# Gated edge terms for two batches at a time, and wider one-hots in the first mean pass, in a four-layer graph network

## The reference, cut to what matters

```python
x = layernorm(x + gated(x, edge_index, edge_attr_64, ...))
x = layernorm(x + mean_sage(x, ...))
x = layernorm(x + gat_twice(x, edge_index, edge_attr_128, ...))
x = layernorm(x + two_mean_layers(x, edge_index, ...))

# gated: a message for each edge, summed by target, divided by the degree
msg_in = concat([h[src], h[dst], e], -1)
m = (silu(msg_in @ w1 + b1) @ w2 + b2) * sigmoid(msg_in @ wg + bg)
agg = segment_sum(m, dst, n) / max(deg, 1)
# mean_sage
agg = segment_sum(feat[src], dst, n) / max(deg, 1)
out = feat @ W_self + b_self + agg @ W_neigh
# each of the two attention layers needs, of every edge
a_e = edge_attr_128 @ We @ att_e
```

## Time and profile before

| | |
|---|---|
| median of 3 runs | 1869.95 us (1869.58 to 1870.87) |
| the profiled execution's own time | 1871.19 us |
| its span | 1869.3 us |
| mean granted TensorE clock | 0.89 |
| TensorE busy | 1563.2 us (84%) |
| VectorE busy | 1479.7 us (79%) |
| ScalarE busy | 1148.4 us (61%) |
| GpSimd busy | 937.0 us (50%) |

### The profile page before, as it was taken

The page is one execution under the profiler, slowest core; times in us unless marked ns, Lnnn a source line. Parts: engine busy times, 40 slices in busy tenths (PEclk is TensorE's granted clock), DMA queues, the critical chain, the costliest instruction groups (busy, mean ns, idle before and its releaser), DMA issues. The chain is left out here.

```text
span 1869.3 us, 43539 instructions
## 1 busy us (share of the span) xinstructions
PE 1563.2 (84%) x13220; PEld 1350.2 (72%) x13220; DVE 1479.7 (79%) x4411; ACT 1148.4 (61%) x2906; POOL 937.0 (50%) x940
## 2 busy tenths in 40 slices
PE   6699999999999846999674899884659989479996
PEld 5488888888888733555573798784649978379995
DVE  5688888888888688999556998756689977668797
ACT  2577677777777537677310998753059976366572
POOL 4777777777777230000054777755567777300000
PEclk9799999999999967999865899996669999689897
DMA  6888888888888300232273211114621111346561
GB/s 199 246 260 247 244 253 264 256 264 256 252 251 262 115 5 36 95 128 116 101 214 74 62 40 42 42 33 126 149 57 44 41 42 42 124 151 243 200 243 37
DMA packets 148928, 273.55 MB, mean 146 GB/s; under 512 B 28039, under 2 KB 88909, under 8 KB 146436
## 3 DMA queue, kind: packets, MB, share of 16 engines
q1 hardware_dynamic: 110430, 192.44, 31.8%
q0 software_dynamic: 33408, 75.68, 15.1%
q10 hardware_dynamic: 4854, 2.55, 0.6%
HBM read 225.06 MB, written 45.51 MB: 145 GB/s over the span
## 5 line engine op out<-in xcount | busy, mean ns | idle before, releaser
L1002 POOL DMA_INDIRECT gated_rows<-p_tab,src_idx x416 | 434.9, 1045 | 152.0 <-issue 121.2
L1410 POOL DMA_INDIRECT cur<-table,src_idx x240 | 247.0, 1029 | 95.0 <-issue 54.5
L1119 ACT ACTIVATE gated_sig<-gated_pre 128x512 f32<-128x512 f32 x208 | 131.4, 632 | 153.6 <-DVE gated_pre L1207 139.8
L1622 PE MATMUL bank<-attention_counts,h_sb 128*128 128x260 f32 (+1 forms) x900 | 216.4, 364 | 0.0
L1043 PE MATMUL bank<-gated_wide_q,gated_comb 128*128 128x256 f32 x832 | 216.0, 382 | 0.0
L2335 PE MATMUL bank<-mean_wide,mean_xs 128*128 128x416 f32 (+2 forms) x900 | 182.3, 360 | 35.1 <-DVE mean_xs L2451 33.0
L1207 DVE TENSOR_TENSOR gated_pre<-bank,gated_rows 128x512 f32<-128x512 f32 x208 | 142.8, 687 | 77.2 <-PE bank L1043 76.6
L2335 PEld LDWEIGHTS bank<-mean_wide,mean_xs 128*128 128x128 f32 x900 | 165.0, 206 | 38.3 <-ACT mean_wide L2293 33.3
L1550 ACT ACTIVATE attention_lo<-attention_plain,w_left 128x128 fp32r<-128x128 bf16 x512 | 177.3, 398 | 14.1 <-DVE attention_plain L1671 13.7
L1571 ACT COPY attention_counts<-bank 128x475 f32 (+1 forms) x256 | 143.8, 562 | 63.0 <-PE bank L1610 59.5
L1605 PE MATMUL bank<-attention_wide_a,attention_lo 128*128 128x300 f32 x512 | 157.5, 391 | 18.7 <-ACT attention_lo L1550 9.6
(11 more groups left out here) (452 smaller groups left out, 4114.6 us busy)
## 6 DMA issues: line engine op xcount, KB each, us to landing
counts<-count_tabs SPq DMA_DIRECT2D x16, 2675.0 KB, 9.4
h_sb<-in_edge_attr_dram SPq DMA_DIRECT2D x51, 512.0 KB
count_tabs<-mean_counts SPq DMA_DIRECT2D x40, 535.0 KB, 2.8
gated_relr<-rel_rows SPq DMA_DIRECT2D x104, 128.0 KB
gated_ids<-id_rows SPq DMA_DIRECT2D x26, 512.0 KB
gated_wide_q<-q_tab SPq DMA_DIRECT2D x208, 64.0 KB
attend_hot_lo<-low_hots SPq DMA_DIRECT2D x52, 256.0 KB, 4.1
gated_ea<-in_edge_attr_dram SPq DMA_DIRECT2D x51, 256.0 KB
```

Source lines behind the costliest of these rows:

```text
L1002: pool.indirect_dma_start(out=rows[:, q % TICKS, c, :], out_offset=None, in_=p_tab, in_offset=bass.IndirectOffsetOnAxis(ap=src_idx[:, b, j ...
L1119: act.activation(flat(sig[:, q % 4, :, :]), flat(pre[:, q % 2, :, :]), ACT.Sigmoid).then_inc(sig_ready, 1)
L1410: pool.indirect_dma_start(out=ring_row(n, j), out_offset=None, in_=table, in_offset=bass.IndirectOffsetOnAxis(ap=src_idx[:, gathered_batch ...
L1622: mm = pe.matmul(BANKS_D[k % 2][:, 0:width], h_sb[:, m, :], counts[:, home(first), m, at:at + width], start=(m == 0), stop=(m == NT - 1), ...
```

## The change

Two parts. In the gated pass a constant `TERMS = 2` makes the edge-term visit come once in four pairs: it then makes the terms of two batches (sixteen records) into two parts of `ST`, and ScalarE copies 256 columns at once. The ring `eaT` grows to 8 pairs; waits and counts follow. In the first mean pass `lo` is made for a batch at a time (one operation with 512 columns in place of two with 256), `onto` for four batches at a time (200 columns in place of four operations with 50); TensorE's matmuls only take their operands from other places.

```diff
-            TRN = 6
+            TRN, TERMS = 8, 2
...
-                        sp.wait_ge(ae_placed, (g + 1) * AG_)
+                        sp.wait_ge(ae_placed, (g + 1) * AG_ // TERMS)
...
-                        if k == PAIRS - 1:
-                            for j in range(J):
-                                pe.matmul(ST[j * AE_COLS:(j + 1) * AE_COLS, 2 * P:3 * P], ae_v[:, :], eaT[:, (q - k + j // 2) % TRN, j % 2, :],
-                                          start=True, stop=True, skip_group_check=True)
+                        if (q + 1) % (TERMS * PAIRS) == 0:
+                            for i in range(TERMS):
+                                for j in range(J):
+                                    pe.matmul(ST[j * AE_COLS:(j + 1) * AE_COLS, (2 + i) * P:(3 + i) * P], ae_v[:, :],
+                                              eaT[:, (q + 1 - (TERMS - i) * PAIRS + j // 2) % TRN, j % 2, :],
+                                              start=True, stop=True, skip_group_check=True)
...
-                        reach(act, s_turned, q - TRN + 2)
+                        reach(act, s_turned, ((q - TRN) // (TERMS * PAIRS) + 1) * TERMS * PAIRS)
...
-                        if k == PAIRS - 1:
+                        if (q + 1) % (TERMS * PAIRS) == 0:
                             reach(act, ae_kept[b // AG_ % 2], 32 * (b // AG_ // 2))
-                            act.copy(ae_rows[:, b // AG_ % 2, b % AG_, :], ST[:, 2 * P:3 * P]).then_inc(ae_placed, 1)
+                            first = b % AG_ + 1 - TERMS
+                            act.copy(flat(ae_rows[:, b // AG_ % 2, first:first + TERMS, :]), ST[:, 2 * P:(2 + TERMS) * P]).then_inc(ae_placed, 1)
...
-            LR, WR, XR, CR = 5, 4, 3, 4
-            lo = sb("lo", [P, LR, 2, P], BF16)
+            LR, WR, XR, CR, OB = 4, 4, 2, 4, 4
+            lo = sb("lo", [P, LR, J, P], BF16)
...
-            onto, zero = sb("onto", [P, XR, PAIRS, NT], BF16), sb("zero", [P, 1])
+            onto, zero = sb("onto", [P, XR, OB, PAIRS, NT], BF16), sb("zero", [P, 1])
...
-                        pe.wait_ge(lo_ready, n + 1)
+                        pe.wait_ge(lo_ready, n // PAIRS + 1)
...
-                            pe.wait_ge(onto_ready, (n - 1) // PAIRS + 1)
+                            pe.wait_ge(onto_ready, (n - 1) // GO + 1)
...
-                    def make_lo(n):
-                        b, k = n // PAIRS, n % PAIRS
-                        reach(dve, counted, n - LR + 2)
+                    def make_lo(b):
+                        reach(dve, counted, PAIRS * (b - LR) + PAIRS + 1)
...
-                    def make_onto(b):
-                        reach(dve, counted, PAIRS * (b - XR) + PAIRS + 1)
+                    def make_onto(q):
+                        reach(dve, counted, GO * (q - XR) + GO + 1)
...
                         if n is not None and n + AHEAD < NDD:
-                            make_lo(n + AHEAD)
+                            if (n + AHEAD) % PAIRS == 0:
+                                make_lo((n + AHEAD) // PAIRS)
                             make_wide(n + AHEAD)
-                            if (n + AHEAD) % PAIRS == 0 and (n + AHEAD) // PAIRS > 1:
-                                make_onto((n + AHEAD) // PAIRS)
+                            if (n + AHEAD) % GO == 0:
+                                make_onto((n + AHEAD) // GO)
```

More of the change, by code:

```diff
@@ L860, in gated_pass @@
             AG_ = 4
+            assert AG_ % TERMS == 0 and NB % AG_ == 0
             ae_rows = sb("ae_rows", [P, 2, AG_, P])
@@ L1836, in mean_build @@
             NDD = NB * PAIRS
+            GO = OB * PAIRS
+            assert NDD % GO == 0
             SELF = {SBP + 5 * g: g for g in range(NG)}
@@ L1961, in _, with low, ahead_of @@
                 def _(pe):
+                    def low(n, c):
+                        return lo[:, n // PAIRS % LR, n % PAIRS * 2 + c, :]
+                    def ahead_of(n):
+                        return onto[:, n // GO % XR, n % GO // PAIRS, n % PAIRS, :]
                     def count(n, at):
-                        pe.wait_ge(lo_ready, n + 1)
+                        pe.wait_ge(lo_ready, n // PAIRS + 1)
                         pe.wait_ge(wide_ready, n + 1)
@@ L1967, in count @@
                         if not opening:
-                            pe.wait_ge(onto_ready, (n - 1) // PAIRS + 1)
-                            pe.matmul(to[:, :, 0], lo[:, (n - 1) % LR, 1, :], onto[:, (n - 1) // PAIRS % XR, (n - 1) % PAIRS, :],
+                            pe.wait_ge(onto_ready, (n - 1) // GO + 1)
+                            pe.matmul(to[:, :, 0], low(n - 1, 1), ahead_of(n - 1),
                                       start=True, stop=False, skip_group_check=True)
-                        pe.matmul(to[:, :, 0:WA], lo[:, n % LR, 0, :], wide_a[:, n % WR, :], start=opening, stop=False, skip_group_check=True)
+                        pe.matmul(to[:, :, 0:WA], low(n, 0), wide_a[:, n % WR, :], start=opening, stop=False, skip_group_check=True)
                         if closes(M_BLOCKS, n):
@@ L1974, in count @@
                             pe.matmul(to[:, :, WA:WP], lo_iota[:, :], blank[:, :], start=False, stop=False, skip_group_check=True)
-                        pe.matmul(to[:, :, bass.ds(at, WA)], lo[:, n % LR, 1, :], wide_b[:, n % WR, :], start=False, stop=True,
+                        pe.matmul(to[:, :, bass.ds(at, WA)], low(n, 1), wide_b[:, n % WR, :], start=False, stop=True,
                                   skip_group_check=True).then_inc(counted, 1)
@@ L2023, in _ @@
                     link = chain(dve, v)
-                    def make_lo(n):
-                        b, k = n // PAIRS, n % PAIRS
-                        reach(dve, counted, n - LR + 2)
-                        dve.tensor_tensor(lo[:, n % LR, :, :], lo_iota[:, :].rearrange("p (a n) -> p a n", a=1).broadcast_to([P, 2, P]),
-                                          src_lo[:, b, 2 * k:2 * k + 2].rearrange("p (j n) -> p j n", n=1).broadcast_to([P, 2, P]),
+                    def make_lo(b):
+                        reach(dve, counted, PAIRS * (b - LR) + PAIRS + 1)
+                        dve.tensor_tensor(lo[:, b % LR, :, :], lo_iota[:, :].rearrange("p (a n) -> p a n", a=1).broadcast_to([P, J, P]),
+                                          src_lo[:, b, :].rearrange("p (j n) -> p j n", n=1).broadcast_to([P, J, P]),
                                           ALU.is_equal).then_inc(lo_ready, 1)
@@ L2036, in make_wide @@
                         dve.tensor_scalar(wide_b[:, n % WR, :], code_iota[:, :], code[:, b, 2 * k + 1:2 * k + 2], None, ALU.is_equal).then_inc(wide_ready, 1)
-                    def make_onto(b):
-                        reach(dve, counted, PAIRS * (b - XR) + PAIRS + 1)
-                        dve.tensor_tensor(onto[:, b % XR, :, :], lo_iota[:, 1:NT + 1].rearrange("p (a n) -> p a n", a=1).broadcast_to([P, PAIRS, NT]),
-                                          next_code[:, b, :].rearrange("p (j n) -> p j n", n=1).broadcast_to([P, PAIRS, NT]),
+                    def make_onto(q):
+                        reach(dve, counted, GO * (q - XR) + GO + 1)
+                        dve.tensor_tensor(onto[:, q % XR, :, :, :],
+                                          lo_iota[:, 1:NT + 1].rearrange("p (a b n) -> p a b n", a=1, b=1).broadcast_to([P, OB, PAIRS, NT]),
+                                          next_code[:, q * OB:(q + 1) * OB, :].rearrange("p b (j n) -> p b j n", n=1).broadcast_to([P, OB, PAIRS, NT]),
                                           ALU.is_equal).then_inc(onto_ready, 1)
@@ L2081, in _ @@
                     for n in range(AHEAD):
-                        make_lo(n)
+                        if n % PAIRS == 0:
+                            make_lo(n // PAIRS)
                         make_wide(n)
                     make_onto(0)
-                    make_onto(1)
                     dve.wait_ge(turned, 1)
```

## The result

The changed kernel takes 1848.98 us in the median, the kernel before 1870.41: a ratio of 0.9889 with a 95% interval of 0.9866 to 0.9912, or 16.5 to 25 us less. The forecast was 1853 in a range of 1846 to 1864. The profiled execution after took 1845.54 us with a span of 1843.7; it lies 3.4 under its median, that of before .8 over its, so I don't take the difference of the two spans, but read each stage by itself. One of the four timed executions of the changed kernel took 2527.23 us at a granted clock of 0.57, where the others had about 0.89; the ratio leaves it out, and without it the median is 1848.95.

The account below looks back on a forecast made before the run. TensorE was taken to bound the gated pass; 13.5 (visits) + 2.2 (stall behind the look) + 1.5 (mean pass) = 17.2 us less, from 1869.95 to 1852.7, said as 1853, range 1846 to 1864.

Parts of the forecast that it names:

- The visit: Gated pass, TensorE's edge-term visit: two batches cost .76 instead of 2 x .51, saving .26 each, 52 times, 13.5 us.
- The stall: Gated pass, TensorE's idle behind VectorE's look: shrinks by .12 in 18 cycles, about 2.2 us, bounds 0 and 6.7.
- The cover: GpSimd in gated pass: gathers issued about seven steps ahead absorb a lag; costs nothing, up to 6 us if failing.
- Rival C: Gated pass: the gathers' lag is not absorbed and GpSimd becomes the bound; 9 us saved, 1861, chance .12.
- B: Gated pass: the second batch costs a whole visit, 1.02 for two, nothing saved there; 6 us saved, 1864, chance .12.
- D: Gated pass: the .33 and .18 idle are a wait that shows again one step on; 1869, chance .06.
- E: Gated pass: each further group waits for the previous matmul and load, .40 instead of .125; about 1877, chance .06.
- The mean part: First mean pass: wider lo and onto save VectorE 13.5 us, mostly hidden; 1.5 us counted, bounds -1 and 13.5.
- TensorE's .81: First mean pass, later blocks: TensorE's regular step of .81 us sets the pace, so VectorE's saving is worth almost nothing.

Follow-up runs that it names:

- copy order run: The changed kernel with ScalarE's copy of the turned silu ahead of the sigmoid in each step instead of behind it: 1842.48 us, ratio 0.9861 to the kernel before.

## Why the prediction was right

*The visit.* Right in mechanism and nearly in size. The term was 52 x .26 = 13.5; the visit is .73 and not .76, since a group costs .11, below both rows that I had taken it from. 48 of the 52 pairs of batches save .29, 13.9 us. The last two cycles show no saving: their 16 pairs take 45.1 us before and 45.2 after. The first of them holds a pause of TensorE that the prediction did not see, in a step of 9.60 us; it is put down to "issue", is as long before (first line) as after (second), and no run shows its cause:

```profile
633.14 0.18 PEld L1030 LDWEIGHTS bank<-ident,gated_ea 128*128 128x128 f32 x1 [5.72 <-issue]
```

```profile
615.65 0.18 PEld L1031 LDWEIGHTS bank<-ident,gated_ea 128*128 128x128 f32 x1 [5.72 <-issue]
```

Over the profiles that cycle takes 29.6 and 30.3 us with the old visit and 28.8 to 29.9 with the new one, too much scatter to read a few tenths. The last eight pairs take .16 more in each of the five profiles with the new visit (15.68 or 15.69 against 15.52 or 15.53). The prediction had counted all 52 pairs of batches at .26; that 13.5 comes so near the measured sum is in part luck, since its two errors, a saving too small and four pairs too many, stand against each other.

*The stall.* 18 x .12 was forecast; it fell from .34 to .25 in the sixteen cycles from pair 64 to 192, 16 x .09 = 1.4. 13.9 + 1.4 = 15.3 is what the trace shows up to pair 192 (533.35 less 518.05); less .2 behind it, 15.1, the measured gain of the pass. The copy order run shows that the chain is the one that the prediction read from the earlier trace rows.

*GpSimd.* The cover held. Its idle did not fall, though the prediction said that it would: it is 124.3 us before 373 gathers against 122.7 before 361; the twelve more fitted in since a gather took 1.012 us in place of 1.048. add_pre's idle, 74.7 us over the span, is put down to TensorE for 73.0, with no gather among the releasers. Rival C is out.

*The rivals B, D and E.* One .33 and one .20 per visit, whether it makes one, two or four batches: B is out. The idle in front of the visits fell from 29.8 to 15.2 us and did not come back in another step: those without a visit are still 2.45. D is out. A further group costs .11 and not .40: E is out.
The rule of the Trainium skill, "TensorE: Matmul & The Clock Gate", Part 3, "The mechanism", that a weight load overlaps matmuls in flight only where it is aimed at other rows, does not describe these tiles: all use the same 128 rows, and yet in the visit of after the second four's loads start at 405.42 and the third four's at 405.53, while the first four's matmuls, begun from 405.39 on and .30 long in the profile, are in flight. That section of the Trainium skill itself makes an exception, which the prediction left out, for a load aimed at the background weight buffer; the trace agrees as far as it goes, since each four's loads begin once the matmuls of the four before have begun, never more than one four ahead; no run shows the buffer itself.

*The mean part.* Here a term was mis-sized: "I take 1.0 there and .5 for all the later blocks' openings: 1.5". It is 4.2: 3.2 in the first block and .7 in the third, with .1 or less in the second and in those behind, where the prediction said that TensorE's .81 hides it. The prices of the operations were right (.60 and .28), so the 13 batches of the first block are 13 x .13 = 1.7 us of VectorE, and I should have kept that whole, since VectorE is busy 58.73 of 65.6 us there. About 1.0 more is something that the prediction didn't see: in this block some operations of VectorE last to the end of an operation of GpSimd. Before there were nine of .9 us or more, after eight; what they last over .3 us each adds up to 8.3 and 7.3 us. Two of them after, with the operations of GpSimd beside them:

```profile
657.63 1.29 DVE L2048 TENSOR_SCALAR mean_wide_a<-code_iota,code 128x300 bf16<-128x300 f16 x1
658.85 1.30 DVE L2049 TENSOR_SCALAR mean_wide_b<-code_iota,code 128x300 bf16<-128x300 f16 x1
```

```profile
657.24 1.59 POOL L1902 TENSOR_TENSOR y_sb<-h_sb,x_sb 128x512 f32<-128x512 f32 x1
658.79 1.26 POOL L1900 TENSOR_TENSOR h_sb<-y_sb,h_sb 128x512 f32<-128x512 f32 x1
660.13 1.26 POOL L1902 TENSOR_TENSOR y_sb<-h_sb,x_sb 128x512 f32<-128x512 f32 x1
```

657.63 + 1.29 = 658.92, just behind GpSimd's 658.83; 658.85 + 1.30 = 660.15, behind 660.05. That GpSimd causes it is shown by the run with the gate on VectorE. That the one long operation less is due to the order in which the wider ones fall beside GpSimd's is argued only; with lo alone there are the same eight, 7.2 us over, so it came with lo. Some .5 us of the first block were not traced to a wait.

The .7 of the third block is VectorE's pace. Before, TensorE waited for it there, and the step was 1.22 in place of .81:

```profile
772.07 0.10 PEld L1969 LDWEIGHTS bank<-mean_onto,mean_lo 128*128 128x128 bf16 x1 [0.64 <-DVE mean_lo L2028]
```

From there to the last pair but one of the block a pair's second wide one-hot (L2036) ended only .25 to .31 us before the last matmul of its count began; after, it is .44 to 1.10, and behind its opening TensorE waits for VectorE nowhere in the block. (The view names lo, which was done at 771.59; the wide one-hot ended at 772.00.) So the prediction's "From 726 on that lies behind TensorE's .81" failed in the third block.

*The sum.* 15.1 + 4.2 = 19.3 by the stages, against 17.2 forecast; the medians say 21.4, with 16.5 to 25 in the interval. The 2 us between stages and medians are within what the stages that no run changes move by.

## What to carry to other kernels

Where an engine pays for a change of shape and not for the work, do more of that work at a time, and take the price from runs at two sizes: here the two numbers from them, .29 and .11, told the third size before it ran (1.17 us forecast, 1.16 measured). A gain on the bounding engine may come back as a stall at the next place where it arrives early; look up what is late there (here ScalarE's order) before counting it. In a block where an engine is nearly full, count its saving whole, and look at the longest of equal operations, not only at their mean.

## What the runs showed of the hardware

- A run of 32-column tiles between full ones cost .29 us once, with 8, 16 or 32 records in it, and a run of 16 full tiles in its place nothing beyond its .112 each. The Trainium skill, "TensorEngine Tiling (Array Packing)", "Key Properties", says that a change of the tiling mode drains the engine; the trace agrees, with its loads idle for .33 us in front of the run and .20 behind it, and gives it this price.
- One-hot operations of VectorE (128x300, bf16 from f16) took .29 us alone and up to 1.30 where they started behind an operation of GpSimd on 128x512 fp32, ending within .1 us of GpSimd's end. One that started .04 us ahead of GpSimd's took .28, and there GpSimd's took 1.36 in place of 1.26:

```profile
661.88 0.28 DVE L2048 TENSOR_SCALAR mean_wide_a<-code_iota,code 128x300 bf16<-128x300 f16 x1
```

```profile
661.92 1.36 POOL L1900 TENSOR_TENSOR h_sb<-y_sb,h_sb 128x512 f32<-128x512 f32 x1 [0.53 <-ACT h_sb L1930]
```

Not every operation of VectorE was held: L2061, which reads a bank, took .34 us beside GpSimd's operations as without them. The Trainium skill, "SBUF — State Buffer", "SBUF: two separate sides", says that these two engines share one pair of ports, which whoever comes first keeps for its whole instruction, and that of VectorE's operations only those in a two-port mode or with two inputs from SBUF take the pair; the trace agrees in who is held and for how long, and does not show the modes.
- Four 32-column tiles side by side cost TensorE .11 us for each of the two records that an fp32 matmul leaves in the trace, as much as one record of a full 128-column tile (.112).
